# Spreading the kept row tiles over every chunk in a graph network's first edge pass

## The reference

```
source_x = jnp.take(node_x, sources, axis=0)
target_x = jnp.take(node_x, targets, axis=0)
message_in = jnp.concatenate((source_x, target_x, edge_x), axis=1)
message_x = _mlp(message_in, msg_W1, msg_b1, msg_W2, msg_b2)
agg = jax.ops.segment_sum(message_x, targets, num_segments=num_nodes)
```

## Time and profile before

| what | value |
|---|---|
| median of 3 runs | 10546.47 us |
| lowest and highest | 10538.37 and 10551.42 us |
| span of the profiled execution | 10555.8 us |
| PE busy | 7991.0 us, 76% |
| DVE busy | 6240.8 us, 59% |
| POOL busy | 4303.7 us, 41% |
| ACT busy | 3471.9 us, 33% |
| first edge pass, from its first gather to the last add of rows | 1034 to 3014 us |
| slot tables and kept gathers | 250 to 1023 us |

### The profile page before, as it was taken

One profiled execution on the slowest core, in us unless ns is written; L12 is line 12 of the kernel. 1 busy time (PEld: TensorE's weight loads), 2 busy tenths in 40 slices (PEclk: granted clock), 3 DMA queues, 4 the chain that ended last, 5 costly groups with the idle time before them and its releaser, 6 DMA issues. The chain is left out here.

```text
span 10555.8 us, 256075 instructions
## 1 busy us (share of the span) xinstructions
PE 7991.0 (76%) x88983; PEld 7100.2 (67%) x88983; DVE 6240.8 (59%) x17891; ACT 3471.9 (33%) x6439; POOL 4303.7 (41%) x3929
## 2 busy tenths in 40 slices
PE   5665666766776999999868887888875777777777
PEld 5443566666666988898757776777754677666676
DVE  4996233333335999999856665566653544544544
ACT  1000122222223666666534443344431222222221
POOL 2887656565610000000023342244323666666663
PEclk9766777777766999999969897788875776777766
DMA  5312222222213223223222221222211111111111
GB/s 66 45 38 48 52 55 55 56 56 55 57 27 83 93 93 94 94 90 92 74 65 77 75 79 56 71 76 76 76 54 23 22 22 22 22 22 22 22 22 24
DMA packets 639193, 594.58 MB, mean 56 GB/s; under 512 B 384326, under 2 KB 488102, under 8 KB 638568
## 3 DMA queue, kind: packets, MB, share of 16 engines
q1 hardware_dynamic: 511192, 436.31, 15.1%
q0 software_dynamic: 125776, 150.49, 7.7%
q10 hardware_dynamic: 1728, 0.25, 0.0%
HBM read 536.45 MB, written 50.23 MB: 56 GB/s over the span
## 5 line engine op out<-in xcount | busy, mean ns | idle before, releaser
L792 POOL DMA_INDIRECT soft_G<-soft,soft_idx x1568 | 1540.4, 982 | 908.1 <-issue 406.8
L792 POOL DMA_INDIRECT msg_G<-msg_src,msg_idx x1176 | 1184.0, 1007 | 779.0 <-issue 325.8
L1755 POOL DMA_INDIRECT sage_chunk_rows<-sage_rows,chunk_src x672 | 842.2, 1253 | 1492.5 <-PE ps L1790 1170.4
L1799 ACT ACTIVATE sage_G<-ps 128x384 bf16<-128x384 f32 (+1 forms) x2100 | 990.6, 485 | 1271.9 <-PE ps L1810 1084.8
L1822 PE MATMUL ps<-sage_G,sage_ohd 128*128 128x192 bf16 x8232 | 1106.9, 260 | 357.1 <-issue 217.8
L1728 DVE TENSOR_SCALAR sage_ohd<-iota,sage_cols 128x256 bf16<-128x256 bf16 x4116 | 941.7, 283 | 725.0 <-PE ps L1822 639.6
L1810 PE MATMUL ps<-T,sage_ohT 128*128 128x192 bf16 x8232 | 1118.4, 261 | 27.9 <-issue 25.6
L662 POOL MEMSET acc<- 96x1280 f32 x30 | 34.4, 1162 | 2604.8 <-POOLq L2148 2288.9
L1602 PE MATMUL ps<-att_far,att_ohT 128*128 128x65 bf16 x15582 | 930.4, 195 | 155.2 <-DVE att_ohT L1541 101.3
L1822 PEld LDWEIGHTS ps<-sage_G,sage_ohd 128*128 128x128 bf16 x8232 | 744.3, 103 | 439.8 <-issue 252.2
L1602 PE MATMUL ps<-acc,att_ohT 128*128 128x65 bf16 x15582 | 929.8, 195 | 17.4 <-issue 17.4
(11 more groups left out here) (459 smaller groups left out, 16987.3 us busy)
## 6 DMA issues: line engine op xcount, KB each, us to landing
sage_rows<-srow SPq DMA_DIRECT2D x336, 320.0 KB
acc<-pair_rows SPq DMA_DIRECT2D x196, 448.0 KB, 3.7
att_rows<-pair_rows SPq DMA_DIRECT2D x147, 448.0 KB
msg_edge<-edge_attr SPq DMA_DIRECT2D x196, 256.0 KB
soft_G<-soft,soft_idx POOLq DMA_INDIRECT x1568
sage_rows<-srow SPq DMA_DIRECT2D x84, 288.0 KB
msg_G<-msg_src,msg_idx POOLq DMA_INDIRECT x1176
kept_rows<-acc POOLq DMA_DIRECT2D x49, 256.0 KB
```

Of the source, the lines that this page charges most:

```text
L792: eng.indirect_dma_start(B["G"][h][:, j, :], None, src_table, bass.IndirectOffsetOnAxis(ap=B["idx"][h][:, j:j + 1], axis=0)).then_inc(gath ...
L1755: pool.indirect_dma_start(chunk_rows[n % 2][:, j, :], None, sage_rows, bass.IndirectOffsetOnAxis(ap=chunk_src[:, n, j:j + 1], axis=0)).the ...
L1799: act.activation(G[s % RING][:, 0:m, :], ps[:, s % RING, 0:m * 3 * D].rearrange("p (c n) -> p c n", c=m), ACT.Copy).then_inc(S["taken"], 1)
```

## The change

The same number of row tiles is kept, but spread: of every chunk the last two tiles (j = 6 and 7) are kept rows, and POOL gathers the other six. `QUADS` is 196 * 2 / 8 = 49 groups of eight kept tiles, each of four chunks. The store of a group writes four blocks of 128 partitions by 512 bytes. SP loads one such block for every chunk, into the last two tiles of its buffer. All consumers of `G` wait for two semaphores. The `paces` of this pass are None, so there is no wait between the six gathers of a chunk. The attention pass keeps its paces, written with a None ahead of them.

```diff
-KEPT = (2, 6)
+KEPT = 2
...
-        kept_rows = dram("kept_rows", (len(kept_chunks), P, TPC * D))
+        QUADS = C * KEPT // TPC
+        kept_rows = dram("kept_rows", (C, P, KEPT * D))
...
-                kept_in = {h: scope.enter_context(nc.semaphore(f"{name}_kept{h}")) for h in kept}
+                kept_in = [scope.enter_context(nc.semaphore(f"{name}_kept{h}")) for h in range(U if kept else 0)]
+                FETCHED = TPC - kept
...
                     def wait_gather(eng, h, turn):
-                        if h in kept:
+                        if kept:
                             eng.wait_ge(kept_in[h], turn * 16)
-                        else:
-                            eng.wait_ge(gathered[h], turn * (16 * TPC))
+                        eng.wait_ge(gathered[h], turn * (16 * FETCHED))
...
                     def gather(eng, c, h, turn):
-                        if h in kept:
-                            return
                         eng.wait_ge(S[rows_user], at(c, U))
                         eng.wait_ge(S["idx"], at(c))
                         hold(eng)
-                        for j in range(TPC):
-                            if j and j % 2 == 0:
-                                user, back = paces[j // 2 - 1]
+                        for j in range(FETCHED):
+                            if j % 2 == 0 and paces[j // 2]:
+                                user, back = paces[j // 2]
...
                                 def load_kept(c, h, turn, last):
-                                    if h in kept:
-                                        sp.wait_ge(S[rows_user], at(c, U))
-                                        hold(sp)
-                                        q = (turn + -1) * len(kept) + kept.index(h)
-                                        sp.dma_start(B["G"][h][:].rearrange("p j d -> p (j d)"), kept_rows[bass.ds(q, 1)].rearrange("o p n -> p (o n)")).then_inc(kept_in[h], 16)
+                                    sp.wait_ge(S[rows_user], at(c, U))
+                                    hold(sp)
+                                    sp.dma_start(B["G"][h][:, FETCHED:TPC, :].rearrange("p j d -> p (j d)"), kept_rows[bass.ds(c, 1)].rearrange("o p n -> p (o n)")).then_inc(kept_in[h], 16)
...
         def store_kept(pool, q):
             pool.wait_ge(gathered[q % KRING], (q // KRING + 1) * (16 * TPC))
-            pool.dma_start(kept_rows[q], kept_G[q % KRING].rearrange("p j d -> p (j d)")).then_inc(stored[q % KRING], 16)
+            per = TPC // KEPT
+            pool.dma_start(kept_rows[q * per:(q + 1) * per].rearrange("c p n -> p c n"), kept_G[q % KRING].rearrange("p (c j) d -> p c (j d)", j=KEPT)).then_inc(stored[q % KRING], 16)
...
-                for j in range(TPC):
-                    pool.indirect_dma_start(kept_G[q % KRING][:, j, :], None, msg_src, bass.IndirectOffsetOnAxis(
-                        ap=srci[:, kept_chunks[q], j:j + 1], axis=0)).then_inc(gathered[q % KRING], 16)
+                for t in range(TPC):
+                    c, j = q * (TPC // KEPT) + t // KEPT, TPC - KEPT + t % KEPT
+                    pool.indirect_dma_start(kept_G[q % KRING][:, t, :], None, msg_src, bass.IndirectOffsetOnAxis(
+                        ap=srci[:, c, j:j + 1], axis=0)).then_inc(gathered[q % KRING], 16)
...
-                  paces=(("sums", U), ("oh_turned", U - 3), ("pre", U - 2)))
+                  paces=(None,) * 3)
...
-                  rows_user="msg", win_user="em", win_table=soft_dst, wcols=1, paces=(("spread", U - 2), ("oh_turned", U - 4), ("sums", U - 1)))
+                  rows_user="msg", win_user="em", win_table=soft_dst, wcols=1, paces=(None, ("spread", U - 2), ("oh_turned", U - 4), ("sums", U - 1)))
```

More of the change, by code:

```diff
@@ L60, in gnn_kernel @@
     TWICE = C * CE - E
-    assert C % 2 == 0 and HALF <= P and TWICE % TPC == 0 and TAIL and E >= CE and (C - 1) * CE < E
+    assert C % 2 == 0 and C * KEPT % TPC == 0 and HALF <= P and TWICE % TPC == 0 and TAIL and E >= CE and (C - 1) * CE < E
     DUP = TWICE // TPC
@@ L92, in gnn_kernel @@
         soft = dram("soft", (NPAD, D + 2))
-        kept_chunks = [c for c in range(C - 1) if c % U in KEPT]
-        kept_rows = dram("kept_rows", (len(kept_chunks), P, TPC * D))
+        QUADS = C * KEPT // TPC
+        kept_rows = dram("kept_rows", (C, P, KEPT * D))
         soft_dst = dram("soft_dst", (NPAD, 1))
@@ L707, in edge_pass @@
         def edge_pass(name, stages, src_table, cols, bufs, programs, rows_user, oh_user="sums", win_user="pre",
-                      last_stage="acc", win_table=None, wcols=0, edges=False, oht=F32, kept=(), paces=()):
+                      last_stage="acc", win_table=None, wcols=0, edges=False, oht=F32, kept=0, paces=()):
             with ExitStack() as scope:
@@ L814, in load_kept @@
                                 def load_kept(c, h, turn, last):
-                                    if h in kept:
-                                        sp.wait_ge(S[rows_user], at(c, U))
-                                        hold(sp)
-                                        q = (turn + -1) * len(kept) + kept.index(h)
-                                        sp.dma_start(B["G"][h][:].rearrange("p j d -> p (j d)"), kept_rows[bass.ds(q, 1)].rearrange("o p n -> p (o n)")).then_inc(kept_in[h], 16)
-                                chunks(sp, (0, load_kept), (2, body))
+                                    sp.wait_ge(S[rows_user], at(c, U))
+                                    hold(sp)
+                                    sp.dma_start(B["G"][h][:, FETCHED:TPC, :].rearrange("p j d -> p (j d)"), kept_rows[bass.ds(c, 1)].rearrange("o p n -> p (o n)")).then_inc(kept_in[h], 16)
+                                chunks(sp, *([(0, load_kept)] if kept else []), (2, body))
                         @block.gpsimd
@@ L845, in _ @@
                         def _(eng):
-                            landed = [(k not in kept) * (C // U + (k < C % U)) * (16 * TPC) for k in range(U)]
+                            landed = [(C // U + (k < C % U)) * (16 * FETCHED) for k in range(U)]
                             for s, n in zip(gathered, landed):
-                                if n:
-                                    eng.wait_ge(s, n)
+                                eng.wait_ge(s, n)
                             eng.inc_swdge_sem(gathered, landed, mode="sub")
@@ L853, in _ @@
                         def _(sp):
-                            for s in [*S.values(), *loaded, *kept_in.values(), s_held]:
+                            for s in [*S.values(), *loaded, *kept_in, s_held]:
                                 sp.sem_clear(s)
@@ L1115, in finish_kept @@
         def finish_kept(pool):
-            for q in range(len(kept_chunks) - 3, len(kept_chunks)):
+            for q in range(QUADS - 3, QUADS):
                 store_kept(pool, q)
-            count = [len(range(k, len(kept_chunks), KRING)) for k in range(KRING)]
+            count = [len(range(k, QUADS, KRING)) for k in range(KRING)]
             for k in range(KRING):
@@ L1311, in _ @@
                             clear_beside(pool)
-                            gather_kept(pool, EARLY[1] + 4, len(kept_chunks))
+                            gather_kept(pool, EARLY[1] + 4, QUADS)
                             finish_kept(pool)
```

## The result

Over five executions each, taken in turn on one chip, the changed kernel takes **10609.44 us** (10579.49 to 10630.32) and the kernel before 10538.37 us (10520.12 to 10551.42). The ratio is 1.0063, with a 95% interval of 1.0048 to 1.0078: **slower by 0.63%**, 71 us, where 10475 us and faster had been forecast. The profiled execution has a span of 10613.0 us, against 10555.8 before, so the two traces lie 57.2 us apart.

What follows compares the result with a forecast made beforehand. The first edge pass was taken as bound by six gathers a chunk, 7.5 us, plus the pauses PE needs for 60 matmuls. 10546 - 122 (grouping) + 49 (stores) = 10473, given as 10475 us, range 10365 to 10630 us.

Steps and rivals of the forecast that it cites:

- The kept loads: SP's queue in the first pass: 196 loads instead of 49, nothing, covered by SP's waiting; up to 49 us if uncovered.
- the second semaphore: DVE's add in the first pass: one more wait a chunk costs nothing, kept rows being asked for six chunks earlier.
- The start: Start of the first pass: 48 gathers before POOL waits for a first add, about as before; within 10 us.
- The stores: Slot stage, POOL's queue: 49 stores of 512 pieces instead of 128, each 1.0 us longer, 49 us more, all exposed.
- the grouping: POOL's gathers in the first pass: runs of six and twelve, 9.4 us a chunk instead of 10.02, 122 us less.
- the paces: First pass: three waits a chunk go; they would only cut the burst again, their cost or use counted in the runs.
- the two patterns: POOL's gathers in the first pass: runs of six at 8.9 us a chunk, runs of twelve at 9.85; middle 9.4.
- My four stretches: First pass before: pauses of 2.8, 2.0, 2.5, 2.3 us with six gathers give 73 matmuls on average in 9.93 us.
- The run of twelve: Two joined bursts in the first pass: 90 matmuls in 17.3 us, 2.4 us more pause, 9.85 us a chunk.
- A: Rival, first pass: runs of six hold, 220 us less, with the stores 10375 us; chance 0.20.
- B: Rival, first pass: each gather costs PE a fixed amount, still 10.02 us a chunk, only stores left, 10595 us; chance 0.24.
- C: Rival, first pass: bursts join without end; three joined take 10.3 us a chunk, 60 us more, 10655 with stores; chance 0.14.

Runs made afterwards that it cites:

- the first set of waits: Changed kernel with old store layout and waits ahead of tile 2 on the sum, tile 4 on the turned one-hot: 10546.15 us, ratio 0.9988.
- after, other waits, old stores: Changed kernel with old store layout and waits ahead of tile 2 on the turned one-hot, tile 4 on the product: 10429.68 us, ratio 0.9886.
- the best kernel: Changed kernel with old stores, waits on turned one-hot and product: 10429.68 us, ratio 0.9886; 0.9984 and 0.9987 on chips without starvation.

## Why the prediction was wrong

**What was right.** On the chips where this holds, PE starves in long runs of gathers and is fed after a pause. Runs became 6 and 12 long: of 106 pauses from 1150 to 2900 us 41 end in a run of six, nearly all others in one of twelve, and runs of 16 or 18 are gone. The kept loads, SP's waits and the second semaphore cost nothing that the trace shows. The start takes 7.7 us more from first gather to first add, within the 10 I allowed. That the first gather is 9.3 us later is the stores ahead of it, 49 x 0.22 = 10.8 us. DVE's wait at the end of the slot stage grew with them, as forecast, from 50.2 to 62.9 us.

**The stores** were the term with the wrong size: 49 us forecast, 10.8 measured. The 512 pieces cost 0.22 us more than 128, 0.6 ns for each further piece, so the low end was near and the middle was not. By the Trainium skill (DMA: Bandwidth & Descriptors, Anatomy of one DMA) the term would be near nothing, and the trace is nearer to that than I was. The stores are not stretched beside DVE either: 777 to 825 ns, all 49 of them, while the gathers among them take 1581 ns on average. So the trap that the Trainium skill describes (SBUF — State Buffer, the "DVE blocks DMA" trap) does not show on these stores. That it is what stretches the gathers is not shown: DVE is busy beside the stretched ones (0.97 of their time), but nearly as much beside the others (0.83). With the stores of before and the first set of waits the ratio is 0.9988, and 1.0024 with the new stores. The difference of 38 us goes the way of the 10.8 but is larger (the nearest ends of the two intervals are 14 us apart). The two ratios are from different chips, and what makes the rest is not shown.

**The step that failed** is the grouping: every further us of pause counted "at the fed rate of 76 in 6 us, 12.7 a us", and with it the paces put at nothing, since they "would only cut the burst again". I worked the two patterns out for the pauses that they would need at that rate. They get other pauses, and PE starts fewer matmuls in them. Cutting 1150 to 2900 us of each trace at every pause over 1.3 us, and each run after its sixth gather, gives (matmuls started in a us, and my own count from the records):

| kernel | pauses: number, total us, matmuls a us | first six gathers: total us, matmuls a us | later gathers: total us, matmuls a us |
|---|---|---|---|
| before | 128, 416, 6.6 | 778, 8.5 | 551, 1.9 |
| after | 106, 436, 5.3 | 808, 8.7 | 504, 1.8 |
| before, no waits | 87, 476, 5.9 | 640, 9.2 | 637, 1.9 |
| after, waits, old stores | 114, 354, 4.8 | 895, 8.6 | 507, 2.5 |
| after, other waits, old stores | 145, 308, 4.5 | 1023, 8.4 | 373, 2.3 |

The last kernel's gathers end at 2853 us, and still it does 182 chunks in its 1704 us where the kernel after does 171 in 1748. In the first six gathers the rate hardly differs from kernel to kernel. In the pauses it does, and what it follows is the run ahead of the pause. Behind a run of nine gathers or more PE starts 3.8 to 4.1 matmuls a us, at a mean granted clock of 0.50 to 0.53 (5.5 at 0.59 in the kernel before without its waits, where these pauses last 6.9 us). Behind a shorter run it starts 5.0 to 8.8, at 0.64 to 0.91.

In a run of six in the kernel after, the pause of 4.73 us on average gives 18 matmuls and the six gathers 65, 83 in all. 40 of these 41 stand behind a run of twelve. My four stretches stood behind runs of 12 and 14, with 2.73 us of idle time on average by the trace. (I had taken 0.30 off each for the usual gap, and my windows lie 1 us late. Counted from the last gather's end they give 70, 65, 80 and 79, as good as the same.) So by my step 4.73 us would give 73 + (4.73 - 2.73) x 12.7 = 98. In the best kernel a run of six has a pause of 2.29 us and gives 8.5 + 60.6 = 69. So **further pause brings about 5 matmuls a us and not 12.7**: 5.0 counted from my own stretches, 5.6 from the best kernel (7.2 from its twelve such runs behind nine gathers or more). The windows show why: behind a starved stretch PE has the lower clock (0.50 in the 5.20 us above, and less than half the matmuls in a busy us), and the 66 of the burst behind come whether the pause was 3.4 or 5.2 us. The run of twelve was right: pause 3.72 us, 24 + 67 + 14 = 105 matmuls, where the step gives 79 + 11 + (3.72 - 2.64) x 12.7 = 104. Of these 65 pauses 40 stand behind a run of six, at a granted clock of 0.92. With my rates, but in the pauses that they had, the 106 pauses and runs would have held 41 x 98 + 65 x 104 = 10778 matmuls, 9.7 us a chunk. They held 10228, which is 10.25.

The four stretches behind my 73 matmuls stand ahead of row tiles 2 and 6, so all four pauses were of the kind that a wait on PE ends. I read from them what PE needs, and took it for what the ring would grant. With the waits gone, a burst is released by an add and nothing else, and the add comes at one of two times: within the running burst, and then six more gathers run into a starved PE, or after PE has recovered at the lower clock and finished a chunk, and then the pause is 4 to 5 us. The paces stop POOL sooner, in the middle of a chunk's gathers, and end the pause at a step of PE itself (the turned one-hot five chunks back, the product six back), with no add, ReLU and index copy behind it. A pause that the ring ends lasts 4.7 us on average in the kernel before (208 us in 44) and 4.1 in the kernel after (436 in 106), and one that a wait between tiles ends 2.5 in the kernel before (200 in 79) and 2.2 in the best (292 in 133). That the waits are worth this much both experiments show, each from its side: waits put back, 10.22 to 9.89 us a chunk; waits taken out, 10.06 to 10.58. Whether it is the shorter pauses or the fewer gathers beyond the sixth that bring it, they do not separate: from the kernel after to the best they fall by 128 and 131 us in the table. Spreading the rows seems to help when waits stay (10.06 to 9.87 and 9.89, on other chips and with two waits instead of three), by a third of what I had put on it. In the whole time little of it is seen, 0.9988 with the old stores and 1.0024 with the new. So the change gave up about 0.33 for 0.19.

**The rivals.** A, runs of six that hold, fell: 41 of 106. B, a fixed budget of pauses, gave 10595 and is nearest to the 10609 measured, but that is luck: its 49 us for the stores, 38 too many, stand where the pass lost time. And its reason fell: the same gathers and matmuls took 9.37, 9.87, 9.94, 10.22 and 10.58 us a chunk, with other grouping, waits and spacing (on several chips). C, joining without end, fell: no third burst joins, for the reason given against it. But two bursts of eight join in the kernel before without its waits, and its 10.58 us a chunk is what that costs. What decided was a fourth thing, what the waits between row tiles do, and none of my cases held it. That it works through the length of the pauses is argued from the table. It had been in sight: POOL's 40 waits on the index copy in the kernel before are 4.8 us on average, and I put that down as an argument for B and priced nothing with it.

## What to carry to other kernels

A wait that looks idle may be pacing a queue that harms another engine, so it is priced by taking it out alone, on the kernel as it is. When such a queue is held back, try releasing it by a step that shows the harmed engine at work again within its chunk, and not by the end of the chunk: here the pauses then came more often and shorter, and 308 us of them did more than 436. Which step matters, too: waits on the turned one-hot and the product took 9.37 us a chunk, waits on the sum and the turned one-hot 9.87, on one chip. A rate read while an engine is fed, at the full granted clock, does not price the time behind a stall.

## What the runs showed of the hardware

**Indirect DMAs in a row hold PE's issue up, and plain DMAs don't.** After the sixth gather PE starts 1.8 to 2.5 matmuls a us in the five traces of the table, where it starts 8.4 to 9.2 in the six before. With plain DMAs of the same bytes, of neighbouring rows, in place of three of the six gathers it starts 95 (from SP's queue) and 108 (from POOL's) in 10 us. Three gathers and 1.34 us for recovery avoid it (9.94 us a chunk, against 9.92 on a chip where nothing starves). How a gather reaches PE's issue is not settled: the waits between PE's own matmuls at line 963 are 0.7 us on average (290.9 us in 394), and the DMA engines are busy for 0.23 of the pass.

**Chips differ in it.** On two chips the starving does not happen at all, and the same kernel before takes 9104 and 9080 us instead of 10530 to 10660. There POOL's six gathers bound the chunk (7.61 to 7.65 us), the waits are worth nothing, and spacing costs 4.7%. What is different in these chips no run shows. The best kernel is no slower there (0.9984 and 0.9987), and 1.1% faster where PE starves.

**A long starve costs twice.** The granted clock falls in the starved half of a run (0.65 in the window above) and is at the lower level, 0.50, in the pause behind a run of twelve, where PE starts 6.0 matmuls a busy us against 12.7 at full clock. In the stretch from 1150 to 1950 us the best kernel has a mean granted clock of 0.81, and the one with three plain DMAs from POOL 1.00. The mean does not rank the kernels: the kernel after has 0.78 and the faster kernel before 0.76.
